# Causal zeroes written by GpSimd in place of mask products on TensorE, with a new order of a step

## The chip, the cores and the metric

The kernel runs on one core of a Trainium2 chip. A core has five engines with queues of their own: TensorE (PE in the profile, its weight loads as PEld), VectorE (DVE), ScalarE (ACT), GpSimd (POOL) and SyncE (SP, which here only starts DMAs). They wait for each other by semaphores. The metric is the device time of one execution in microseconds, lower is better. The time before is the median of three runs, 595.81 us (594.65 to 596.34).

## The reference

Eight sequences of 256 tokens with 128 channels go through a block of two attentions and a mixture of experts:

```python
x = _layernorm(x + _L0_attn_ref(x, Wq, bq, Wk, bk, Wv, bv, Wo, bo))     # attention A
x = _layernorm(x + _L0_ffn_ref(x, ...))                                 # attention B, then experts

# attention A: 16 query heads of 8 channels, one key head, one value head
att = jnp.einsum('bthd,bThd->bhtT', q, k) / math.sqrt(HD)
causal = jnp.triu(jnp.ones((Tx, Tx), bool), 1)
att = jnp.where(causal, -jnp.inf, att)
att = jax.nn.softmax(att, axis=-1)
out = jnp.einsum('bhtT,bThd->bthd', att, v).reshape(Bx, Tx, Cx)
return out @ Wo + bo
```

Attention B has 16 query heads of 64 channels and 4 key and value heads, also causal. The experts (8, the two best of each token routed, with a capacity) follow it. Only the causal mask of attention A is touched by the change: a key later than its query must get the probability 0.

## The kernel before

**Steps and stages.** The eight sequences go through a software pipeline of twelve steps, numbered -4 to 7. A step holds pieces of up to eight stages, each for another sequence: PA (projections and rotation of attention A), MA (row maxima of its scores), SA (its scores, exponentials and values), TA (its output, residual and norm), and PB, MB, SB and TB, which do the like for attention B. Steps 0 to 3 hold nearly all of them; PA ends with step 3, MA and SA with step 4, PB with step 5. The twelve steps end at about 500 us; a loop over 15 groups of expert tiles follows.

**Attention A of one sequence.** The score matrix of 256 x 256 per head is cut into three blocks, keys by queries: DIAG0 (the first 128 keys and queries), OFF (first keys, last queries), DIAG1 (last keys and queries). Later keys exist only in DIAG0 and DIAG1. `maxima_a` computes the masked scores with the queries on partitions, twelve tiles `am0` to `am11`, and VectorE reduces each to row maxima. `max_rows_a` transposes the maxima (`nm0`, `nm1`), ScalarE negates them, and a DMA writes them as an extra row of the query operand. `scores_a(s, c)` then computes block c transposed, keys on partitions, into all four banks of `ps_st`: four products of 25 rows (L700), one per group of four heads, that carry the negated maximum. For DIAG0 and DIAG1, four products of an identity with a key mask (L697) are accumulated ahead of them, which put -1e30 where the key is later. `exp_a` on ScalarE (L1691, two calls of 128 x 1024 per block, chunks 0 to 5) turns them into probabilities in `pt`; `values_a(s, 0)` (DIAG0) and `values_a(s, 1)` (OFF and DIAG1) multiply them with the values and a column of ones (L715).

**What sets the order.** Every engine's queue is written by hand in its function `step(s)`. TensorE's outputs other than scores go into a ring of four banks of `ps_r`, in the order of the table `ORDER`: each fill waits until the fill four places before it was read out by its reader, ScalarE or VectorE. So ORDER says both what TensorE does next and which reader it waits for. The names in it: `p00` to `p02` and `p10` to `p12` are the projections of attention B's queries and keys for the two halves of a sequence (L957), which VectorE's `rotate` reads; `r00` to `r12` their transposes (L966), which ScalarE's `high_parts` and then VectorE's `split` read; `bm0` to `bm11` the maxima tiles of attention B (L905, L909), `nmT` their transpose (L917); `bv0` to `bv3` its values (L930), `sm0`, `sm1` its weights (L946); `ax` and `qkv` the transposed input and projection of attention A (L670, L751); `av0`, `av1` the values of attention A (L715); `qT0`, `qT1`, `kT0`, `kT1` its transposed queries and keys (L765, L771); `xfT`, `lg` the router's (L813, L821).

**GpSimd.** Its queue per step: the product with the inverse sums (L592), `add_rotary` for both halves (L555, three additions each, one after each of `rotate`'s three parts), `spread_a` (L539 to L547, which `qT0` waits for) and copies.

Of the kernel before, what the change touches and what calls it, by code (L numbers as in the profile page):

```python
# [27 lines left out]
ALU = mybir.AluOpType  # L28
# [3 lines left out]
P = 128  # L32
# [156 lines left out]
def build(nc, x, Wq, bq, Wk, bk, Wv, bv, Wo, bo, g1, g2, wq, wk, wv, wo, router_w, router_b,  # L189
          w1, w2, w3, cf, cb, out):  # L190
    with ExitStack() as ctx:
# [192 lines left out]
        probs_a, probs_b = sem("probs_a"), sem("probs_b")  # L384
        xn_in = sem("xn_in")
# [134 lines left out]
        def _(pool):  # L520
# [35 lines left out]

            def scatter(i, lo, hi, src):
# [29 lines left out]
            for s in range(FIRST, NB):  # L587
# [7 lines left out]
                if "PB" in on:  # L595
                    add_rotary(s, 0)
                    add_rotary(s, 1)
                if "PA" in on:
                    spread_a(s + AHEAD["PA"])
                if s == FIRST:  # L600
# [45 lines left out]
        def _(pe):  # L646
# [38 lines left out]
            def scores_a(s, c):  # L685
# [10 lines left out]
                for a in range(4) if kind != OFF else ():  # L696
                    nc.tensor.matmul(o[a], ident_b, kmask.unsqueeze(1).broadcast_to([P, 4, P]), start=True, stop=False)  # L697
                for a in range(4):
                    rows = slice(RG * a, RG * a + NROW + 1)
                    mm = nc.tensor.matmul(o[a], kta[rows, a, P * kt:P * (kt + 1)], qta[rows, :, P * qt:P * (qt + 1)],  # L700
                                          start=kind == OFF, stop=True, tile_position=(RG * a, 0))
# [3 lines left out]
            def values_a(s, qt):  # L705
# [5 lines left out]
                pe.wait_ge(probs_a, E_A * n + (2 if qt == 0 else E_A))  # L711
                blocks = [(DIAG0, 0)] if qt == 0 else [(OFF, 0), (DIAG1, 1)]
# [257 lines left out]
            def step(s):  # L970
# [49 lines left out]
                if "PB" in on:  # L1020
                    project(s, 0)
                if s == NB - 1:
# [6 lines left out]
                else:  # L1029
                    values(s, 3)  # L1030
                    weights(s, 1)
                maxima_a(s, 10, 12)
                max_rows_a(s, 1)
                maxima(s, 8, 10)
                if "PB" in on:
                    project(s, 1)
                if "PA" in on:
                    n = s + AHEAD["PA"]
                    turn_x(s, "ax", x_all[:, NT * n:NT * (n + 1), :])
                if "SA" in on:  # L1040
                    scores_a(s, 0)
                maxima(s, 10, 12)
# [872 lines left out]
```

## Time and profile before

| what | value |
|---|---|
| median of three runs | 595.81 us (594.65 to 596.34) |
| the profiled execution, time / span | 594.53 us / 592.6 us |
| PE busy | 481.7 us (81%), 2788 instructions |
| DVE busy | 383.7 us (65%) |
| ACT busy | 229.4 us (39%) |
| POOL busy | 160.6 us (27%) |
| mean granted TensorE clock | 0.947 of full |
| chain that ended last | PE 56%, DVE 20%, ACT 12%, issue 4%, DMA 4%, POOL 3% |

The span runs from the first to the last instruction; 1.9 us of the time lie around it. A busy TensorE is not TensorE at its peak, since matmuls overlap. The granted clock has two levels, 1.2 and 2.4 GHz: 0.5 and 1.0 of full. The idle time of an engine that nobody waits for costs nothing, so what counts is who waited for whom, stretch by stretch.

### The profile page before, as it was taken

The numbers are of one execution on the slowest core, as the hardware profiler recorded it, in microseconds if no ns is written. First come the engines' busy times: TensorE is split into PE (matmuls) and PEld (weight loads), VectorE is DVE, ScalarE is ACT, GpSimd is POOL, SyncE is SP. The second block draws the span as 40 slices with busy tenths as digits, with TensorE's granted clock in tenths as the row PEclk, the third lists the DMA queues.
The fourth block names the chain that finished last, engine by engine and source line by source line (L and its number), as shares of the span: only waits on it lengthen the run. The fifth ranks groups of instructions, "written<-read, shape, count | busy, mean of one in ns | idle before, by whom it ended". The sixth has DMA issues, their size and how long they took to land.

```text
span 592.6 us, 8112 instructions
## 1 busy us (share of the span) xinstructions
PE 481.7 (81%) x2788; PEld 265.9 (45%) x2788; DVE 383.7 (65%) x1096; ACT 229.4 (39%) x420; POOL 160.6 (27%) x200
## 2 busy tenths in 40 slices
PE   3766686799979989997998799889967889898910
PEld 2423353355345535453653456344543535565610
DVE  3508678657857674857577666847678634675775
ACT  1251350374274238324641743264242232445400
POOL 4210601400323031324022420403223634033531
PEclk9977997899999999999999999989988989999965
DMA  7400000000002002100300030003043162013223
GB/s 212 148 1 1 1 1 2 2 1 1 3 3 71 2 3 52 23 2 2 73 2 2 2 73 2 2 3 71 2 144 72 47 147 72 2 59 98 70 50 85
DMA packets 19093, 23.82 MB, mean 40 GB/s; under 512 B 2630, under 2 KB 15374, under 8 KB 18158
## 3 DMA queue, kind: packets, MB, share of 16 engines
q1 hardware_dynamic: 15308, 18.19, 11.4%
q0 software_dynamic: 1648, 4.07, 2.7%
q10 hardware_dynamic: 2098, 1.05, 0.6%
q8 instruction: 23, 0.38, 0.3%
q14 instruction: 16, 0.13, 0.1%
HBM read 16.71 MB, written 6.28 MB: 39 GB/s over the span
## 4 chain that ended last, share of the span: by engine, by line
PE 56%; DVE 20%; ACT 12%; issue 4%; DMA 4%; POOL 3%; ACTq 1%; POOLq 0%; DVEq 0%; SPq 0%
PE ps_r L930 8%; PE ps_st L895 6%; ACT pt L1691 6%; PE ps_r L715 4%; PE ps_r L804 4%; PE ps_r L662 4%; PE ps_r L957 4%; PE ps_st L884 4%; DVE rmax L1194 4%; DVE rmax_a L1194 3%; PE ps_r L946 3%; DMA pt<-ys_dram,gidx 3%; PE ps_r L785 3%; POOL qkr L555 2%; PE ps_st L1096 2%
## 5 line engine op out<-in xcount | busy, mean ns | idle before, releaser
L555 POOL TENSOR_TENSOR qkr<-qkr,prod 128x512 f32<-128x512 f32 (+1 forms) x48 | 52.2, 1093 | 208.1 <-DVE prod L1310 207.0
L1194 DVE TENSOR_REDUCE rmax_a<-ps_r 128x2 f32<-128x512 f32 (+1 forms) x96 | 61.7, 686 | 26.1 <-PE ps_r L785 25.6
L662 PE MATMUL ps_r<-cbt 128*128 128x256 bf16 (+1 forms) x192 | 62.9, 327 | 4.9 <-DVE rmax_a L1194 2.4
L1194 DVE TENSOR_REDUCE rmax<-ps_r 128x2 f32<-128x512 f32 (+1 forms) x96 | 61.5, 684 | 4.9 <-PE ps_r L909 4.6
L592 POOL TENSOR_TENSOR oT<-pvb,oT 128x1024 f32<-128x1024 f32 x14 | 33.0, 2374 | 108.2 <-DMA oT<-inv_dram 108.2
L1700 ACT ACTIVATE pt<-ps_st 128x1024 f32<-128x1024 f32 x48 | 47.2, 1022 | 36.0 <-PE ps_st L895 36.0
L930 PE MATMUL ps_r<-pt,vb 128*64 128x512 f32 x192 | 48.9, 617 | 4.7 <-ACT pt L1700 3.0
L1691 ACT ACTIVATE pt<-ps_st 128x1024 f32<-128x1024 f32 x48 | 46.5, 1023 | 13.1 <-PE ps_st L700 12.8
L957 PE MATMUL ps_r<-wqkv,xT_b 128*128 128x512 f32 x96 | 47.6, 635 | 3.2 <-DVE rmax_a L1194 3.2
L785 PE MATMUL ps_r<-kq_a 128*128 128x512 f32 x96 | 46.7, 545 | 0.0
L1322 DVE TENSOR_TENSOR qbuf<-ps_r,qbuf 128x512 fp32r<-128x512 f32 x32 | 20.7, 687 | 34.1 <-ACT qbuf L1775 34.0
L1757 ACT ACTIVATE pvb<-ps_r 128x512 f32<-128x512 f32 x32 | 19.0, 595 | 59.3 <-PE ps_r L930 59.3
L662 PEld LDWEIGHTS ps_r<-cbt 128*128 128x128 bf16 x192 | 18.9, 98 | 48.6 <-issue 31.2
L895 PE MATMUL ps_st<-qbuf,kbuf 64*128 64x512 f32 x288 | 40.6, 415 | 0.0
L715 PE MATMUL ps_r<-pt,va 128*32 128x512 f32 x192 | 26.4, 655 | 9.3 <-ACT pt L1691 9.3
L895 PEld LDWEIGHTS ps_st<-qbuf,kbuf 64*128 64x128 f32 x288 | 25.9, 189 | 14.9 <-issue 10.6
L1307 DVE TENSOR_TENSOR qkr<-ps_r,cft 128x512 f32<-128x512 f32 (+1 forms) x48 | 28.5, 595 | 4.0 <-PE ps_r L957 4.0
L957 PEld LDWEIGHTS ps_r<-wqkv,xT_b 128*128 128x128 f32 x96 | 19.3, 206 | 22.3 <-issue 19.5
L909 PE MATMUL ps_r<-kbuf,qbuf 128*128 128x512 f32 x64 | 27.5, 488 | 0.0
L1248 DVE RECIPROCAL rda<-ps_r 128x16 f32<-128x16 f32 x16 | 4.0, 253 | 35.3 <-PE ps_r L728 35.3
L884 PE MATMUL ps_st<-nrow,cbt 128*128 128x512 bf16 x96 | 25.5, 389 | 1.3 <-DMA nrow<-negmax 1.3
L804 PE MATMUL ps_r<-wob,oT 128*128 128x128 f32 x224 | 26.4, 276 | 0.0
(237 smaller groups left out, 914.9 us busy)
## 6 DMA issues: line engine op xcount, KB each, us to landing
oT<-inv_dram SPq DMA_DIRECT2D x14, 512.0 KB, 6.3
xs_dram<-pvb SPq DMA_DIRECT2D x1, 2048.0 KB
pt<-in_L_ffn_w SPq DMA_DIRECT2D x2, 1024.0 KB, 7.2
ys_dram<-qkr SPq DMA_DIRECT2D x14, 128.0 KB
qkr<-xs_dram POOLq DMA_DIRECT2D x4, 256.0 KB, 5.8
x_all<-in_L_attn_x ACTq DMA_DIRECT2D x1, 896.0 KB, 6.3
pvb<-xs_dram POOLq DMA_DIRECT2D x3, 256.0 KB, 4.0
out<-x_all SPq DMA_DIRECT2D x1, 640.0 KB, 3.9
```

Of the source, the lines that this page charges most:

```text
L555: nc.gpsimd.tensor_tensor(part, part, prod[:, (3 * t + i) % 2, 0:w], ALU.add).then_inc(add_in, 1)
L662: nc.tensor.matmul(o[:, :, P * (i >= 4):], ident_b, qmask.unsqueeze(1).broadcast_to([P, heads, P]), start=True, stop=False, skip_group_che ...
L715: mm = nc.tensor.matmul(o[RG * a:RG * (a + 1), :], va[n % 2][:, kt, :], pt_a(kind)[:, 4 * a:4 * a + 4, :], start=i == 0, stop=i == len(blo ...
L785: nc.tensor.matmul(o, q, k, start=False, stop=True, skip_group_check=True).then_inc(full, 1)
L804: mm = nc.tensor.matmul(o[:, 0:C], of, wob[:, j, :], start=j == 0, stop=j == H // 2 - 1)
L884: nc.tensor.matmul(o[b], top_row if kind == OFF else add_row, nrow[:, G * hk:G * (hk + 1), P * qt:P * (qt + 1)], start=True, stop=False)
L895: mm = nc.tensor.matmul(o[b], k, q, start=False, stop=ql, tile_position=(DB * b, 0))
L930: mm = nc.tensor.matmul(o[DB * b:DB * (b + 1), :], vb[s % 2][:, kt, hk, :], pt_b(kind)[:, G * hk:G * (hk + 1), :], start=j == 0, stop=j == ...
L957: nc.tensor.matmul(o, xT_b[:, P * t:P * (t + 1)], wqkv[:, 512 * i:512 * (i + 1)], start=True, stop=True).then_inc(full, 1)
L1194: nc.vector.tensor_reduce(heads_of(i), ps_r[:, b, :].rearrange("p (h k) -> p h k", h=4 if i < 4 else 2), AX.X, ALU.max).then_inc(free[b], 1)
L1691: nc.scalar.activation(pt_a(kind)[:, 8 * half:8 * half + 8, :], ps_st[:, c % 2, :, :].rearrange("p b (h t) -> p (b h) t", h=4), ACT.Exp, s ...
L1700: nc.scalar.activation(pt_b(kind)[:, 8 * half:8 * half + 8, :], ps_st[:, c % 2, :, :].rearrange("p b (h t) -> p (b h) t", h=4), ACT.Exp, s ...
```

## The change

The eight mask products per sequence (L697, 64 in all) are left out; the first product of each bank now starts the accumulation. Two instructions of GpSimd per sequence, `affine_select` over 128 x 2048 elements in `pt`, keep a probability where the query index is at least the key index and write 0 elsewhere. They come after the exponentials of DIAG0 and of DIAG1 and before the values that read them, with a new semaphore `causal_in`. In GpSimd's queue the first stands between the two halves of `add_rotary`, the second behind `spread_a`.

The order of a step is changed with it: `scores_a(s, 0)` goes from behind `ax` to behind `p02`; `am10`, `am11` and `nm1` go ahead of `bv3` and `sm1`; `bm10`, `bm11` come together with `bm8`, `bm9` ahead of `p10`; `nmT` and `av0` stand ahead of `qkv`; and `av1` stands behind `kT1`, as the last of the step.

```diff
-         ("PB", "p00"), ("PB", "p01"), ("PB", "p02"), ("SB", "bv3"), ("SB", "sm1"),
...
+         ("PB", "p00"), ("PB", "p01"), ("PB", "p02"), ("MA", "am10"), ("MA", "am11"), ("SB", "bv3"), ("MA", "nm1"),
...
@@ gpsimd
+            def keep_causal(s, c):
+
+                pool.wait_ge(probs_a, E_A * (s + AHEAD["SA"]) + 2 * c + 2)
+                probs = pt_a(KINDS_A[c])
+                nc.gpsimd.affine_select(probs, probs, [[0, H], [1, P]], ALU.is_ge, 0.0, base=0, channel_multiplier=-1) \
+                    .then_inc(causal_in, 1)
+
...
                 if "PB" in on:
                     add_rotary(s, 0)
+                if "SA" in on:
+                    keep_causal(s, 0)
+                if "PB" in on:
                     add_rotary(s, 1)
                 if "PA" in on:
                     spread_a(s + AHEAD["PA"])
+                if "SA" in on:
+                    keep_causal(s, 2)
@@ tensor, scores_a
-                for a in range(4) if kind != OFF else ():
-                    nc.tensor.matmul(o[a], ident_b, kmask.unsqueeze(1).broadcast_to([P, 4, P]), start=True, stop=False)
...
-                                          start=kind == OFF, stop=True, tile_position=(RG * a, 0))
+                                          start=True, stop=True, tile_position=(RG * a, 0))
@@ tensor, values_a
                 pe.wait_ge(probs_a, E_A * n + (2 if qt == 0 else E_A))
+                pe.wait_ge(causal_in, 2 * n + 1 + qt)
@@ tensor, step
                     project(s, 0)
+                if "SA" in on:
+                    scores_a(s, 0)
+                maxima_a(s, 10, 12)
...
                     values(s, 3)
+                    max_rows_a(s, 1)
                     weights(s, 1)
-                maxima_a(s, 10, 12)
-                max_rows_a(s, 1)
-                maxima(s, 8, 10)
+                maxima(s, 8, 12)
...
                     turn_qk(s, 1)
+                if "PA" in on:
+                    turn_qk_a(s)
                 if "SA" in on:
                     values_a(s, 1)
-                if "PA" in on:
-                    turn_qk_a(s)
@@ vector, step
-                maxima(s, 8, 10)
+                maxima(s, 8, 12)
                 if "PB" in on:
                     rotate(s, 1)
-                maxima(s, 10, 12)
@@ scalar, step
+                if "SA" in on:
+                    exp_a(s, 0)
+                    exp_a(s, 1)
                 take_values(s, 3)
...
+                neg_max_a(s, 1)
                 take_weights(s, 1)
-                neg_max_a(s, 1)
+                if "MB" in on:
+                    neg_max(s)
```

The line numbers of the changed kernel are 11 or 12 higher from `scores_a` on: L710 is L700, L726 is L715, L968 is L957, L674 is L662, L1205 is L1194.

**The middle of a step.** TensorE's queue in step 1 before, from the last product of `bm9` over `p10` to `p12`, `ax`, the first scores of attention A, `bm10`, `bm11` and `nmT`:

```order
L909 MATMUL ps_r<-kbuf,qbuf 128x512
L957 MATMUL ps_r<-wqkv,xT_b 128x512 x3
L670 MATMUL ps_r<-cft,x_all 128x128 x2
L697 MATMUL ps_st<-cbt 128x512 x4
L700 MATMUL ps_st<-kq_a 128x512 x4
L662 MATMUL ps_r<-cbt 128x2x128
```

And in the changed kernel, in the same step, from `p00` to `p02` over the first scores, `am10`, `am11`, `bv3` and `nm1` to `sm1`:

```order
L968 MATMUL ps_r<-wqkv,xT_b 128x512 x3
L710 MATMUL ps_st<-kq_a 128x512 x4
L674 MATMUL ps_r<-cbt 128x2x128
L796 MATMUL ps_r<-kq_a 128x512
L674 MATMUL ps_r<-cbt 128x2x128
L796 MATMUL ps_r<-kq_a 128x512
L941 MATMUL ps_r<-pt,vb 64x512 x4
L803 MATMUL ps_r<-cft,rmax_a 16x128
L957 MATMUL ps_r<-pt,cft 32x512 x8
```

The scores now follow the first half's projections and have no mask products ahead of them.

VectorE's queue before, at the end of `rotate` for the second half:

```order
L1310 TENSOR_TENSOR prod<-ps_r,cft 128x8x32
L1306 COPY qkr<-ps_r 128x256
L1307 TENSOR_TENSOR qkr<-ps_r,cft 128x256
L1309 TENSOR_TENSOR prod<-ps_r,cft 128x4x32
L1310 TENSOR_TENSOR prod<-ps_r,cft 128x4x32
L1194 TENSOR_REDUCE rmax<-ps_r 128x2 x2
L1232 TENSOR_TENSOR flat<-ps_r,cft 128x272
```

In the changed kernel, at the start of the same `rotate`:

```order
L1404 SCALAR_TENSOR_TENSOR xf<-y,root_t_r,g2b 128x128 x2
L1205 TENSOR_REDUCE rmax<-ps_r 128x2 x4
L1318 TENSOR_TENSOR qkr<-ps_r,cft 128x512
L1320 TENSOR_TENSOR prod<-ps_r,cft 128x8x32
L1321 TENSOR_TENSOR prod<-ps_r,cft 128x8x32
```

All four reductions of `bm8` to `bm11` now stand ahead of `rotate`; before, two of them stood behind it.

**The end of a step.** TensorE's queue before, from the router's last product to the next step's first (L966 are `r10` to `r12`, L715 is `av1`, L765 and L771 are `qT0` to `kT1`, L884 opens the scores of attention B):

```order
L823 MATMUL ps_r<-bias,ones 128x8
L966 MATMUL ps_r<-cft,qkr 128x128 x10
L715 MATMUL ps_r<-pt,va 32x512 x8
L765 MATMUL ps_r<-cft,flat 128x128 x8
L771 MATMUL ps_r<-cft,kz 128x128 x8
L884 MATMUL ps_st<-nrow,cbt 128x512 x4
```

And in the changed kernel:

```order
L834 MATMUL ps_r<-bias,ones 128x8
L977 MATMUL ps_r<-cft,qkr 128x128 x10
L776 MATMUL ps_r<-cft,flat 128x128 x8
L782 MATMUL ps_r<-cft,kz 128x128 x8
L726 MATMUL ps_r<-pt,va 32x512 x8
L895 MATMUL ps_st<-nrow,cbt 128x512 x4
```

`av1` has moved behind the four transposes, so the next step's first scores stand right behind it.

**GpSimd.** Its queue in step 1 before:

```order
L592 TENSOR_TENSOR oT<-pvb,oT 128x1024 x2
L555 TENSOR_TENSOR qkr<-qkr,prod 128x512 x2
L555 TENSOR_TENSOR qkr<-qkr,prod 128x256
L555 TENSOR_TENSOR qkr<-qkr,prod 128x512 x2
L555 TENSOR_TENSOR qkr<-qkr,prod 128x256
L539 TENSOR_TENSOR flat<-qkr_a,hr 128x32x8
L542 COPY flat<-hr 128x32x8 x2
L546 COPY kz<-hr 128x8x8 x2
L547 TENSOR_TENSOR kz<-qkr_a,hr 128x8x8
L611 COPY vb<-qkr 128x512
```

And in the changed kernel:

```order
L555 TENSOR_TENSOR qkr<-qkr,prod 128x256
L561 AFFINE_SELECT pt<-pt 128x2048
L555 TENSOR_TENSOR qkr<-qkr,prod 128x512 x2
L555 TENSOR_TENSOR qkr<-qkr,prod 128x256
L539 TENSOR_TENSOR flat<-qkr_a,hr 128x32x8
L542 COPY flat<-hr 128x32x8 x2
L546 COPY kz<-hr 128x8x8 x2
L547 TENSOR_TENSOR kz<-qkr_a,hr 128x8x8
L561 AFFINE_SELECT pt<-pt 128x2048
L623 COPY vb<-qkr 128x512
```

The two selects are new; nothing else of GpSimd's moved against each other.

## Rows read from the trace of the kernel before

**Rows 1.** The page: busy time and share of each engine; granted clock in 40 slices.
```profile
PE 481.7 (81%) x2788; PEld 265.9 (45%) x2788; DVE 383.7 (65%) x1096; ACT 229.4 (39%) x420; POOL 160.6 (27%) x200
...

```

**Rows 2.** Windows, step 1: length, busy of PE, PEld, DVE, ACT, POOL, clock, DMA.
```profile
176.30:231.80 55.50, 50.24 (x311) 27.40 (x310) 37.91 (x103) 25.10 (x48) 14.16 (x16) 1.00 0.09 21
```

**Rows 3.** Groups by form, the mask products: busy us, mean ns, idle before.
```profile
L697 PE MATMUL ps_st<-cbt 128*128 128x512 bf16 x64 | 16.7, 384 | 7.8 <-ACT pt L1691 7.8
```

**Rows 4.** TensorE's timeline in step 1: start us, us, instructions [idle before <-releaser].
```profile
203.68 2.81 PE L957 MATMUL ps_r<-wqkv,xT_b 128*128 128x512 f32 x6 [0.80 <-DVE rmax_a L1194]
206.42 1.94 PE L930 MATMUL ps_r<-pt,vb 128*64 128x512 f32 x8
...
212.14 0.27 PE L792 MATMUL ps_r<-cft,rmax_a 128*16 128x128 f32 x1 [1.12 <-DVE rmax_a L1194]
...
215.74 1.03 PE L697 MATMUL ps_st<-cbt 128*128 128x512 bf16 x4
216.70 0.51 PE L700 MATMUL ps_st<-kq_a 25*128 25x512 f32 x4
...
219.72 0.27 PE L917 MATMUL ps_r<-cft,rmax 128*32 128x128 f32 x1 [1.70 <-DVE rmax L1194]
219.84 0.48 PE L751 MATMUL ps_r<-wa,xT_a 128*128 128x144 f32 x2
...
224.51 1.04 PE L697 MATMUL ps_st<-cbt 128*128 128x512 bf16 x4 [0.87 <-ACT pt L1691]
...
228.17 1.92 PE L715 MATMUL ps_r<-pt,va 128*32 128x512 f32 x16 [0.45 <-ACT pt L1691]
230.03 1.09 PE L765 MATMUL ps_r<-cft,flat 128*128 128x128 f32 x8
...
231.83 1.03 PE L884 MATMUL ps_st<-nrow,cbt 128*128 128x512 bf16 x4
```

**Rows 5.** VectorE's timeline in step 1.
```profile
208.91 0.28 DVE L1310 TENSOR_TENSOR prod<-ps_r,cft 128x128 f32<-128x128 f32 x1
...
213.22 1.28 DVE L1194 TENSOR_REDUCE rmax<-ps_r 128x2 f32<-128x512 f32 x2
...
218.09 0.28 DVE L1310 TENSOR_TENSOR prod<-ps_r,cft 128x128 f32<-128x128 f32 x1
```

**Rows 6.** ScalarE's timeline in step 1.
```profile
222.52 1.94 ACT L1691 ACTIVATE pt<-ps_st 128x1024 f32<-128x1024 f32 x2
...
227.91 1.10 ACT L1775 ACTIVATE qbuf<-ps_r 128x512 fp32r<-128x512 f32 x2
228.86 0.78 ACT L1779 ACTIVATE kbuf<-ps_r 64x256 fp32r<-64x256 f32 x2
```

**Rows 7.** GpSimd's groups by form.
```profile
L555 POOL TENSOR_TENSOR qkr<-qkr,prod 128x512 f32<-128x512 f32 x32 | 40.6, 1276 | 207.0 <-DVE prod L1310 207.0
L592 POOL TENSOR_TENSOR oT<-pvb,oT 128x1024 f32<-128x1024 f32 x14 | 33.0, 2374 | 108.2 <-DMA oT<-inv_dram 108.2
...
L542 POOL COPY flat<-hr 128x256 f32<-128x256 f32 x16 | 5.9, 398 | 0.0
...
L611 POOL COPY vb<-qkr 128x512 f32<-128x512 f32 x8 | 4.9, 610 | 0.1
```

**Rows 8.** TensorE's timeline in steps -3, -2, 4 and 5.
```profile
34.22 1.26 PE L697 MATMUL ps_st<-cbt 128*128 128x512 bf16 x4 [2.10 <-ACT pt L1691]
...
38.33 3.58 PE L715 MATMUL ps_r<-pt,va 128*32 128x512 f32 x16 [2.12 <-ACT pt L1691]
...
70.32 1.06 PE L715 MATMUL ps_r<-pt,va 128*32 128x512 f32 x8 [1.26 <-ACT pt L1691]
...
386.17 0.27 PE L917 MATMUL ps_r<-cft,rmax 128*32 128x128 f32 x1 [1.92 <-DVE rmax L1194]
...
434.02 0.27 PE L917 MATMUL ps_r<-cft,rmax 128*32 128x128 f32 x1 [3.37 <-DVE rmax L1194]
```

More of the change, by code:

```diff
@@ L384, in build @@
         probs_a, probs_b = sem("probs_a"), sem("probs_b")
+        causal_in = sem("causal_in")
         xn_in = sem("xn_in")
@@ L1030, in step @@
                     values(s, 3)
+                    max_rows_a(s, 1)
                     weights(s, 1)
-                maxima_a(s, 10, 12)
-                max_rows_a(s, 1)
-                maxima(s, 8, 10)
+                maxima(s, 8, 12)
                 if "PB" in on:
                     project(s, 1)
+                if "MB" in on:
+                    max_rows(s)
                 if "PA" in on:
@@ L1040, in step @@
                 if "SA" in on:
-                    scores_a(s, 0)
-                maxima(s, 10, 12)
-                if "MB" in on:
-                    max_rows(s)
+                    values_a(s, 0)
                 if "PA" in on:
@@ L1049, in step @@
                 if "SA" in on:
-                    values_a(s, 0)
                     scores_a(s, 1)
@@ L1395, in step @@
                     ins.then_inc(xf_in, 1)
-                maxima(s, 8, 10)
+                maxima(s, 8, 12)
                 if "PB" in on:
                     rotate(s, 1)
-                maxima(s, 10, 12)
                 if "PA" in on:
@@ L1822, in step @@
                     inverse_root(root_t, var_t, ln_t, r0_t, NB)
+                neg_max_a(s, 1)
                 take_weights(s, 1)
-                neg_max_a(s, 1)
+                if "MB" in on:
+                    neg_max(s)
                 if "PA" in on:
@@ L1827, in step @@
                 if "SA" in on:
-                    exp_a(s, 0)
-                    exp_a(s, 1)
-                if "MB" in on:
-                    neg_max(s)
+                    take_values_a(s, 0)
                 if "TB" in on and s < NB - 1:
@@ L1834, in step @@
                 if "SA" in on:
-                    take_values_a(s, 0)
                     exp_a(s, 2)
@@ L1844, in step @@
                     high_parts(s, 1)
-                if "SA" in on:
-                    take_values_a(s, 1)
                 if "PA" in on:
@@ L1849, in step @@
                     turned_a(s, "kT", kta)
+                if "SA" in on:
+                    take_values_a(s, 1)
             def weigh(lo, hi, count):
```

9 rows, old and new, of the table ORDER are left out of this document.

## The prediction

> **What bounds the kernel now.** Read three views, from wide to narrow. The page first: TensorE is busy for 81% of the span, and its clock is at full in the slices of the middle steps and below it in some of the early ones and of the tail [rows 1]. The windows next: in step 1, TensorE is busy for 50.2 of 55.5 us at a clock of 1.00, VectorE for 37.9, GpSimd for 14.2 [rows 2]. So steps 0 to 3 look bound by TensorE, and whatever leaves its queue should come off the time. The timeline shows what the shares hide: the last third of a step is a braid. TensorE waits there for VectorE before `nm1` (1.12 us) and before `nmT` (1.70), and for ScalarE before the third scores (0.87) and `av1` (0.45) [rows 4]. These are the places that the change touches, so it is these waits that say how much of a removed product is a gain.
>
> **The mask products.** There are 64, in 16 groups of four. A group starts 0.96 us before the scores that follow it (215.74 to 216.70, [rows 4]), so 16 x 0.96 = 15.4 us leave TensorE's queue; the group's line has 16.7 us of busy time, since matmuls overlap [rows 3]. That is the upper end of the gain, if no other engine is next.
>
> **The selects.** What adds 16 instructions to GpSimd is cheap for the engine, 27% busy [rows 1], but no row shows `affine_select`. Bounds for 128 x 2048: the copies take 398 ns for 256 elements and 610 for 512, so 0.83 ns per element and 0.61 + 1536 x 0.00083 = 1.9 us; the two-input products take 1276 ns for 512 and 2374 for 1024, so 2.14 ns per element and 2.37 + 1024 x 0.00214 = 4.6 us [rows 7]. A select reads one tensor as a copy does, so I take 2.0 us, call it X, and keep 1.9 to 4.6. The first select of a step stands behind `add_rotary` of the first half, and has until `av0`, some 8 us; it is hidden for any X. The second select is not: it can start only after the last exponential of DIAG1, and `av1` needs it.
>
> The Trainium skill, page "GPSIMD Engine Reference", section "Performance pitfalls for Q7 kernels", speaks against my X: a compare-and-select loop that isn't unrolled costs 2.03 cycles per element, unrolled 1.03. An estimate by that page with its 1.2 GHz is 3.5 us or 1.8 us; the sum below would then be near -1 us or -9 us. No row here shows which.
>
> **The middle of a step (step 1).** I replay the queues with the durations of the rows. `p02` ends and `bv3` starts at 206.4 [rows 4]. The new queue: first scores until 206.8 (0.43), `am10` and `am11` until 207.7, a short wait for `p01`'s bank, `bv3` until 209.8. `nm1` needs the maxima of `am10`, `am11`, which VectorE starts when `rotate` of the first half ends at 209.2 [rows 5] and ends 1.2 later: 210.5. `sm1` (1.85) until 212.5, `bm8` to `bm11` (0.36 each) until 214.0, the second half's projections (2.7, as the first half's from 203.68 [rows 4]) until 216.7. VectorE waits for `bm8` until 213.0, does the four reductions (0.60 each) until 215.4 and `rotate` (it started 1.20 after 213.22 and ended at 218.37, so 3.95 [rows 5]) until 219.4. `qkv` takes the bank of `p12`, so it starts at 219.5; before it did so at 219.84 [rows 4]. So the first mask group, the shorter wait at `nm1` and the vanished wait at `nmT` bring 0.3 us together, not 1 to 3: VectorE's `rotate` is next, and it now has two more reductions ahead of it. In step 0, which lacks the router's work, the same working gives 0.1 us later than before.
>
> **The end of a step.** Counted from the start Q of `qkv`. ScalarE is the bound: its exponentials of OFF started at Q + 2.7 and the six read-outs of the second half's transposes at 5.4 us behind them [rows 6]. Now `av0` is no longer between, and the exponentials start at Q + 1.6; the chain of exponentials (1.8), read-outs (1.8), exponentials (1.8) brings the last exponential's end to Q + 7.1, the read-outs to Q + 7.0 to 8.7 and VectorE's last split 1 us later, Q + 9.7. `qT1`, `kT0` and `kT1` take the banks of `r10` to `r12`, so `kT1` ends at Q + 10.2 in place of the earlier end of `av1`; `av1` (1.86) comes last. It starts at Q + 10.2 or Q + 7.2 + X, whichever is later, and ends at Q + 12.1 for X up to 3.0. Before, the step ended at 231.83, Q + 12.0 [rows 4]. So the second mask group gains nothing in steps 1 to 3 either: what TensorE saves, it waits for banks. Sum for steps 0 to 3: +0.1 - 3 x 0.25 = -0.7 us. Beyond X = 3.0 each of these steps loses X - 3.0, since the select delays `av1`, and behind it the next step's scores.
>
> **The other steps.** Here the order pays. Step -2: the exponentials of DIAG0 were waited for (1.26 us at 70.32 [rows 8]); with the scores ahead of the second half's projections that is hidden, and by the same replay the step ends 1.7 us earlier. Step -1: `qkv` is freed of the wait for VectorE and comes 1.7 us earlier, and so does the end. Step 4 has no `qkv`: the scores of OFF can follow `av0` at once, 3.7 us earlier; the last part is then bound by ScalarE and the select, and ends at 393.0 + X against 396.94 before: -2.1 at X = 1.9, and TensorE no longer waits 1.92 us for VectorE at `nmT` [rows 8]. Step 5 has no attention A scores, but the wait of 3.37 us at `nmT` [rows 8] goes, since the four reductions are ahead of `rotate`; `rotate` is late instead and holds `r01`: -1.8. Step -3 has nothing to hide the selects behind, and its waits for exponentials are 2.10 and 2.12 us [rows 8]; both X lie on the path: with 5 us less of waits and masks than before and 2 X more, -1.4 at X = 1.9. From step 5 on nothing else changes and the shift is carried to the end.
>
> **The sum** at X = 1.9: -1.4 - 1.7 - 1.7 - 0.7 - 2.1 - 1.8 = -9.4; at X = 2.0 it is -9.1. The slope is 3 us per us of X up to 3.0 (step -3 twice, step 4), then 9 (steps -2 to 3 as well): -6.1 at 3.0, 0 near 3.7, +8 at 4.6. The sum goes against the profiled execution's 594.53 us (span 592.6 and 1.9 around it): 585.4. That execution is 1.3 us below the median of 595.81, so for a median I say 587.0.
>
> **Rivals.**
> *TensorE is the bound after all.* If my hand replay puts too much behind VectorE and ScalarE, the 15.4 us come off whole, and step 5's 1.8: 578.6. For it: 50.2 of 55.5 us busy [rows 2]. Against it: the waits in exactly these stretches [rows 4].
> *The select is slow.* X at 4.6, the two-input row: `av1` waits 1.6 us in each of steps -2 to 3, more in -3: 595.8 + 8 = 604, slower than before; it decides from X = 3.7 on. For it: the select also makes an index and compares. Against it: one input.
> *The gains cancel.* X of 3.3 to 3.9, or the clock. TensorE's clock fell to its lower level, 1.2 GHz, after waits: `av1` of step -3 took 3.58 us in place of 1.92 after two waits of 2.1 us [rows 8]. At the end of a step TensorE now has some 1.9 us of waits before `qT1` to `kT1`, so the clock could fall there, and the four score products and `av1` behind would take some 2 us more; in four steps that is 8 us and leaves 594 to 597. Against it: single waits of 1.70 us left the clock at 1.00 [rows 2, 4]. The Trainium skill, page "TensorE: Matmul & The Clock Gate", section "HAM oscillation — how this bites in real kernels", says that recurring waits bring the clock down in every round; by it the time would be in this case, and the row at 38.33 agrees.
> *The change does nothing to the path*: the early steps gain, but the tail, bound by routing, waits for other things; then some 594. Nothing in the rows speaks for it.
>
> **Chances.** Forecast (select near a copy, 583 to 591): 0.50. TensorE is the bound (577 to 583): 0.12. Cancelled (591 to 598): 0.23. Slow select (598 to 606): 0.15. A run can tell about 0.3%, 1.8 us, from no change. Faster: 0.50 + 0.12 + 0.06 of the cancelled = 0.68; same 0.12; slower 0.05 + 0.15 = 0.20. The range from 580 to 600 leaves out some 0.17 of the ends.
>
> **What would show it.** The select's duration, 1.9 to 3.0 us. Step 1's `qkv` some 13.1 us behind the end of `p02`, with VectorE's `rotate` as the releaser; waits of TensorE before `qT1` and `kT1` for VectorE; `av1` waiting for GpSimd not at all in steps 0 to 3, by about 1 to 3 us in step 4; no wait at `nmT` anywhere; steps 1 to 3 still near 55.3 us; clock 1.00 there. I am wrong if steps 1 to 3 take below 54.5 (TensorE was the bound) or above 56 (select or clock).

## The result, and the profile after

The changed kernel takes 604.58 us (median of four runs, 602.17 to 607.69) against 596.08 us for the kernel before: 1.0149 of its time, 95% interval 1.0098 to 1.0200. It is slower by some 1.5%, where the forecast was 587.0 us and the range ended at 600. Its profiled execution took 602.17 us, with a span of 600.3 us against 592.6 us. The ratios here and below leave out the slow runs, those over 1.5% above the fastest of their kernel, and are not the quotients of the medians beside them, from which they differ by up to 0.7%.

The page of the changed kernel, beside [rows 1]: the 64 products are gone (2788 to 2724), yet TensorE is busy for longer. The second line is the granted clock in 40 slices, the third the same of the kernel before.

```profile
PE 486.5 (81%) x2724; PEld 264.8 (44%) x2724; DVE 387.3 (65%) x1096; ACT 231.5 (39%) x420; POOL 193.4 (32%) x216
...
PEclk9957987889989999999799999979988989999965
...
PEclk9977997899999999999999999989988989999965
```

The line of the selects among GpSimd's groups, beside [rows 7]:

```profile
L561 POOL TENSOR_SCALAR_AFFINE_SELECT pt<-pt 128x2048 f32<-128x2048 f32 x16 | 32.1, 2004 | 29.2 <-ACT pt L1701 29.2
```

X, the price of one select, is 2.0 us, the value taken. So the forecast did not fall with its most doubtful number. Where the span grew shows in the starts of the steps, each taken from TensorE's timeline at the first product of attention B's scores:

| start of step | 0 | 1 | 2 | 3 | 4 | 5 | 6 | 7 | end |
|---|---|---|---|---|---|---|---|---|---|
| before, us | 126.1 | 176.3 | 231.8 | 287.3 | 342.8 | 396.9 | 438.9 | 475.0 | 592.6 |
| after, us | 127.7 | 179.6 | 235.1 | 292.2 | 347.6 | 401.7 | 443.5 | 481.8 | 600.3 |
| later by | 1.6 | 3.3 | 3.2 | 4.8 | 4.8 | 4.8 | 4.5 | 6.8 | 7.7 |

The windows of the changed kernel, steps 0 to 4 (columns as in [rows 2], the clock ahead of the last two):

```profile
127.70:179.60 51.90, 46.72 (x265) 22.86 (x261) 33.94 (x88) 24.71 (x43) 13.06 (x15) 0.97 0.02 3
179.60:235.10 55.50, 49.92 (x306) 26.51 (x303) 38.66 (x103) 25.30 (x46) 18.10 (x18) 1.00 0.09 20
235.10:292.20 57.10, 52.25 (x306) 28.33 (x303) 39.53 (x103) 25.40 (x46) 18.10 (x18) 0.94 0.10 22
292.20:347.60 55.40, 49.82 (x305) 26.44 (x301) 38.23 (x103) 25.39 (x46) 18.11 (x18) 1.00 0.08 19
347.60:401.70 54.10, 48.16 (x281) 24.19 (x277) 37.70 (x97) 22.62 (x41) 16.08 (x12) 0.96 0.09 21
```

Steps 1 and 3 take 55.4 us at a clock of 1.00, as long as before [rows 2]: 8 products fewer, and nothing off the time. Steps 0 and 2 hold the same work as before and as their neighbour, but at 0.97 and 0.94, and each is some 1.7 us longer than the kernel before needed (50.3 and 55.5 us). TensorE's timeline at the end of step 1 and of step 2 shows one and the same row of instructions at the two levels of the clock, beside [rows 4]:

```profile
229.33 0.63 PE L776 MATMUL ps_r<-cft,flat 128*128 128x128 f32 x4
231.25 0.66 PE L776 MATMUL ps_r<-cft,flat 128*128 128x128 f32 x4 [1.30 <-DVE qbuf L1333]
231.85 1.42 PE L782 MATMUL ps_r<-cft,kz 128*128 128x128 f32 x8
233.20 1.92 PE L726 MATMUL ps_r<-pt,va 128*32 128x512 f32 x16
235.06 0.82 PE L895 MATMUL ps_st<-nrow,cbt 128*128 128x512 bf16 x3
...
284.95 1.06 PE L776 MATMUL ps_r<-cft,flat 128*128 128x128 f32 x4
286.69 1.11 PE L776 MATMUL ps_r<-cft,flat 128*128 128x128 f32 x4 [0.67 <-DVE qbuf L1333]
287.60 1.91 PE L782 MATMUL ps_r<-cft,kz 128*128 128x128 f32 x8
289.44 2.79 PE L726 MATMUL ps_r<-pt,va 128*32 128x512 f32 x16
```

`av1` (L726) needs 1.92 us in step 1 and 2.79 in step 2, part of it at 1.2 GHz. In step -3, where little else runs beside the selects, and in step 4, the selects stand on the path as well; the middle line is the wait of the products that read `av1`'s result, at the start of step -2:

```profile
29.81 1.94 PE L726 MATMUL ps_r<-pt,va 128*32 128x512 f32 x8 [1.79 <-POOL pt L561]
...
44.27 1.06 PE L739 MATMUL ps_r<-cft,pvs 128*128 128x128 f32 x8 [0.80 <-ACT pvs L1753]
...
398.15 3.64 PE L726 MATMUL ps_r<-pt,va 128*32 128x512 f32 x16 [2.73 <-POOL pt L561]
```

In step 4 the wait for the select is 2.73 us, within the 1 to 3 us foreseen, and the `av1` behind it takes 3.64 us in place of 1.92: the wait is paid twice.

### The profile page after: what moved, and what is told of

It reads as the page before. It is cut to its first block, busy times and chain, and to the rows that moved or that the text cites. A ratio compares the mean times of both kernels' runs of the same rounds, so it can differ in the third digit from the quotient of the medians.

```text
span 600.3 us, 8009 instructions
## 1 busy us (share of the span) xinstructions
PE 486.5 (81%) x2724; PEld 264.8 (44%) x2724; DVE 387.3 (65%) x1096; ACT 231.5 (39%) x420; POOL 193.4 (32%) x216
## 4 chain that ended last, share of the span: by engine, by line
PE 49%; DVE 24%; ACT 10%; issue 6%; POOL 5%; DMA 5%; ACTq 1%; POOLq 0%; DVEq 0%; SPq 0%
PE ps_st L906 6%; PE ps_r L941 6%; ACT pt L1701 5%; PE ps_r L815 4%; PE ps_st L895 4%; PE ps_r L674 4%; PE ps_r L726 4%; DVE rmax L1205 4%; POOL qkr L555 3%; DMA pt<-ys_dram,gidx 3%; DVE rmax_a L1205 3%; PE ps_r L796 2%; DVE qkr L1318 2%; PE ps_r L957 2%; PE ps_st L1107 2%
## 5 line engine op out<-in xcount | busy, mean ns | idle before, releaser
L1205 DVE TENSOR_REDUCE rmax_a<-ps_r 128x2 f32<-128x512 f32 (+1 forms) x96 | 61.8, 686 | 21.1 <-PE ps_r L796 20.7
L674 PE MATMUL ps_r<-cbt 128*128 128x256 bf16 (+1 forms) x192 | 63.7, 332 | 4.2 <-DVE rmax_a L1205 2.3
L1205 DVE TENSOR_REDUCE rmax<-ps_r 128x2 f32<-128x512 f32 (+1 forms) x96 | 60.9, 684 | 5.2 <-PE ps_r L920 4.3
L968 PE MATMUL ps_r<-wqkv,xT_b 128*128 128x512 f32 x96 | 46.8, 626 | 3.8 <-DVE rmax_a L1205 3.2
L561 POOL TENSOR_SCALAR_AFFINE_SELECT pt<-pt 128x2048 f32<-128x2048 f32 x16 | 32.1, 2004 | 29.2 <-ACT pt L1701 29.2
L674 PEld LDWEIGHTS ps_r<-cbt 128*128 128x128 bf16 x192 | 19.0, 99 | 48.3 <-issue 32.0
L726 PE MATMUL ps_r<-pt,va 128*32 128x512 f32 x192 | 30.2, 742 | 8.5 <-POOL pt L561 4.7
L1333 DVE TENSOR_TENSOR qbuf<-ps_r,qbuf 128x512 fp32r<-128x512 f32 x32 | 20.8, 687 | 20.8 <-ACT qbuf L1785 20.7
L906 PEld LDWEIGHTS ps_st<-qbuf,kbuf 64*128 64x128 f32 x288 | 26.1, 191 | 15.6 <-issue 11.2
L895 PE MATMUL ps_st<-nrow,cbt 128*128 128x512 bf16 x96 | 27.2, 410 | 3.1 <-DMA nrow<-negmax 3.1
L968 PEld LDWEIGHTS ps_r<-wqkv,xT_b 128*128 128x128 f32 x96 | 18.8, 205 | 22.6 <-issue 16.4
L977 PE MATMUL ps_r<-cft,qkr 128*128 128x128 f32 x160 | 25.2, 293 | 3.7 <-DVE prod L1321 2.3
```

The lines of the kernel that those rows point to most:

```text
L674: nc.tensor.matmul(o[:, :, P * (i >= 4):], ident_b, qmask.unsqueeze(1).broadcast_to([P, heads, P]), start=True, stop=False, skip_group_che ...
L726: mm = nc.tensor.matmul(o[RG * a:RG * (a + 1), :], va[n % 2][:, kt, :], pt_a(kind)[:, 4 * a:4 * a + 4, :], start=i == 0, stop=i == len(blo ...
L895: nc.tensor.matmul(o[b], top_row if kind == OFF else add_row, nrow[:, G * hk:G * (hk + 1), P * qt:P * (qt + 1)], start=True, stop=False)
L906: mm = nc.tensor.matmul(o[b], k, q, start=False, stop=ql, tile_position=(DB * b, 0))
L968: nc.tensor.matmul(o, xT_b[:, P * t:P * (t + 1)], wqkv[:, 512 * i:512 * (i + 1)], start=True, stop=True).then_inc(full, 1)
L1205: nc.vector.tensor_reduce(heads_of(i), ps_r[:, b, :].rearrange("p (h k) -> p h k", h=4 if i < 4 else 2), AX.X, ALU.max).then_inc(free[b], 1)
```

## The experiments

Two theories went in. **Waits**: each of the three parts (order, masks, selects) moves waits, and those add up. **Clock**: the mask products, useless as work, kept TensorE's clock at its upper level through the waits around them; without them it falls. The kernels were run in four batches (x, y, z, w; y and w on one chip, x and z on two others), each batch with the kernel before, and the ratios are to that. x1, x3, z3 and z4 leave out the causal mask of attention A, so their results are not the reference's. In batches y and w the kernel before itself had medians of 599.5 and 600.3 us, so times of different batches are not compared.

**The parts one by one.** x1 takes the masks out of the kernel before; x2 has the new order, masks, no selects; x3 has the new order and neither; x4 is the changed kernel with more work for TensorE ahead of `qT1`'s wait. y1 is the changed kernel with the mask products put back as well.

```diff
# x1: before, without
-                for a in range(4) if kind != OFF else ():
-                    nc.tensor.matmul(o[a], ident_b, kmask..., start=True, stop=False)
# x2, x3: after, without
-                    keep_causal(s, 0)
-                    keep_causal(s, 2)
-                pe.wait_ge(causal_in, 2 * n + 1 + qt)
# x4: after, qT0's four transposes issued four times
+                    for b in 4 * list(range(4)) if t == 0 else range(4):
```

> The kernel before, in its old order, without the 64 mask products and without selects (later keys keep their probabilities, so the causal mask of attention A is left out). Theory A (the end of a step is bound by ScalarE's exponentials and the banks, the middle by VectorE, so TensorE's saving turns into waits): steps 0 to 3 keep their 50.3 and 55.5 us, only steps -3 to -1 and 4 gain some 1 us each; 591 to 594 us. Rival B (TensorE is the bound, and it is the new order that lost the gain): 15 us off, 580 to 583 us.

> The new order with the 64 mask products kept and no selects: the reordering alone. If the order and the clock behind it are the loss (theory A: TensorE waits at the end of a step, its clock falls to the lower level, av1 behind it takes 2.7 to 3.6 us in place of 1.9), this stays slower than before, 599 to 605 us. If the selects are the loss (rival C), it is at or below before, 590 to 596 us.

> The changed kernel without its 16 selects (the causal mask is left out). The difference from the changed kernel's 604.6 us is the whole price of the selects. Theory A: they are on the path only in steps -3 and 4 (and by 2.7 us there): 598 to 601 us. Rival C (each second select delays av1): below 594 us.

> The changed kernel with the four transposes of qT0 done four times over (12 more transposes of 128 x 128 per sequence, some 1.3 us of TensorE each step, 96 in all), in front of the wait of 1.5 us before qT1. Theory A (the waits at the end of a step let the clock fall): the clock stays at 1.00 in steps -1 to 3, av1 goes back to 1.9 us, and the time falls in spite of more work, to 599 to 602 us. Rival (the clock has nothing to do with these waits): the same 604.6 us, or up to 10 us more.

| kernel | median, us | ratio to before (95%) |
|---|---|---|
| x1, old order, no masks, no selects | 601.35 | 1.0114 (1.0071 to 1.0157) |
| x2, new order, masks, no selects | 582.73 | 0.9811 (0.9788 to 0.9833) |
| x3, new order, no masks, no selects | 596.28 | 1.0035 (1.0004 to 1.0067) |
| x4, after, `qT0` repeated | 599.13 | 1.0118 (1.0092 to 1.0144) |

The first three went against what I expected of them, and together they turn the case over. The order alone is worth 1.9%, and taking the products out costs time in either order: 1.1% in the old one, some 2.3% in the new one. x1's trace shows how. Its step 3, in TensorE's timeline:

```profile
331.31 0.37 PE L915 MATMUL ps_r<-cft,rmax 128*32 128x128 f32 x1 [2.13 <-DVE rmax L1192]
331.47 0.78 PE L749 MATMUL ps_r<-wa,xT_a 128*128 128x144 f32 x2
...
333.42 1.94 PE L713 MATMUL ps_r<-pt,va 128*32 128x512 f32 x8
335.29 0.80 PE L698 MATMUL ps_st<-kq_a 25*128 25x512 f32 x4
```

The product that is gone has become a longer wait for VectorE at `nmT`, 2.13 us where [rows 4] has 1.70, and behind it everything runs at half speed: `av0` (L713) takes 1.94 us for eight products that took 1.07 before, the four score products 0.80 in place of 0.51. Nearly the same wait, 2.12 us, in its step 1 left the clock up, and that step took 55.5 us; steps 2 and 3 took 56.5 and 57.5. So the fall is not certain at any one wait; it becomes likelier.

In x4 the repeated transposes cover the wait at `qT1`, and in its profile (span 593.5 us) the clock is at 1.00 in steps 0, 2 and 3; but that execution was among the shortest of six (594.3 to 601.7 us), and the ratio of all six, 1.0118, is hardly below what the changed kernel itself has (1.0124 and 1.0149). By its time x4 settles nothing; its trace has what I expected of `av1`, 1.92 to 1.93 us in all steps from -3 to 3.

**Old order with selects.** y2 keeps the old order, in which `av1` is followed by `qT0` to `kT1`, and gives it the selects, without the mask products; the first select stands there behind `add_rotary` of both halves.

> The changed kernel, selects and order as they are, with the 64 mask products back (they are superfluous: both mask the same keys, and the result is the reference's). Theory A (without the products TensorE waits more, its clock falls to 1.2 GHz at the ends of the steps and half-speed products cost more than the removed ones): adding 16 us of products takes time off, 604.6 us on the chip of the first comparison becomes 586 to 592 us. Rival (what the changed kernel loses is the selects' waits, and the products only cost): 604 us or more.

> The masking alone in the old order: no mask products, 16 selects, the first behind add_rotary of the second half, the second behind spread_a. Correct result, so no other tokens go to the experts than before. The run without products and selects in this order took 601.4 us. Theory A: the same loss to the clock, and av1 in its old place waits some 2 us for each second select: 606 to 616 us. Rival (the 601.4 us came from the unmasked data, not from the clock): 593 to 603 us.

y2 takes 647.84 us, 1.0820 (1.0701 to 1.0939), far beyond what I had reckoned. TensorE's timeline at the end of its step 1:

```profile
251.37 3.64 PE L726 MATMUL ps_r<-pt,va 128*32 128x512 f32 x16 [2.73 <-POOL pt L562]
254.95 1.87 PE L776 MATMUL ps_r<-cft,flat 128*128 128x128 f32 x8
```

Steps 1 to 3 end as step 4 of the changed kernel does, with a wait of 2.73 us and an `av1` at half speed, and `qT0` and `qT1` behind it take 1.87 us in place of 1.09 [rows 4]: a step takes some 61.6 us at a clock of 0.91 to 0.92. `av0` waits for no select in step 1. In the changed kernel `av1`, as the last of the step, waits for none in these steps, as the forecast had it. That its place is what makes the selects bearable fits these rows, but no run moves `av1` alone with the selects in.

y1 (600.42 us, 1.0086, 1.0036 to 1.0137) stayed above my range, by the ratio as well. The masks back in, its steps 0 to 3 run at 1.00, 1 to 3 in 55.4 us each, but step 4 is hardly helped (53.6 against 54.1 us). The medians of all runs of this batch (599.48 for the kernel before) give 1.0016, and so does the repeat in batch z.

**The clock, with the data held fixed.** z4 is the sharpest test: x3 with the mask products issued, each of them closed and then overwritten by the scores, so that it computes what x3 computes and differs in TensorE's load alone.

```diff
# z4: x3, and ahead of the scores of DIAG0 and DIAG1
+                    nc.tensor.matmul(o[a], ident_b, kmask..., start=True, stop=True)
```

> The changed kernel once more, beside the three below, since chips and runs differ by some us: ratio to before 1.010 to 1.020 as in the first comparison.

> The changed kernel with the mask products kept beside the selects, once more. Theory A (the products keep the clock up at the ends of the steps): below the run without them by 4 to 8 us, ratio 1.000 to 1.009. Rival (the earlier difference was between chips): the same ratio as the run without them.

> New order, no mask products, no selects (the causal mask of attention A is left out), once more: ratio 1.000 to 1.007, with runs apart by up to 8 us according to the step in which the clock falls.

> As the run before and with the same data, but the 64 mask products are issued and then overwritten by the score products (start=True on both), so the causal mask of attention A is left out here too, and only TensorE's work differs. With the products as real masks this order gave 0.981. Theory A (their work keeps the clock): 0.978 to 0.985. Rival (the unmasked data sends other tokens to the experts and costs the time): as the run before, 1.000 to 1.007.

All four in one batch (before: 594.74 us):

| | mask products gone | mask products issued |
|---|---|---|
| **no selects** | z3: 596.25, 1.0021 (0.9987 to 1.0055) | z4: 584.68, 0.9826 (0.9769 to 0.9883) |
| **selects** | z1: 603.88, 1.0124 (1.0074 to 1.0175) | z2: 596.49, 1.0016 (0.9985 to 1.0048) |

16.5 us of dead work on TensorE take 11.6 us off the time. `av1`, always the same 16 products, shows step by step where the clock was down (us, from the timelines; 1.92 is full speed):

| step | -3 | -2 | -1 | 0 | 1 | 2 | 3 | 4 | step 0 starts at |
|---|---|---|---|---|---|---|---|---|---|
| before | 3.58 | 1.92 | 1.92 | 1.92 | 1.92 | 1.92 | 1.92 | 1.92 | 126.1 |
| changed kernel | 2.37 | 2.06 | 3.42 | 2.69 | 1.92 | 2.79 | 1.92 | 3.64 | 127.7 |
| the same again (z1) | 2.12 | 2.81 | 1.92 | 2.02 | 2.86 | 1.92 | 2.88 | 3.51 | 126.7 |
| z3 | 2.64 | 2.18 | 3.56 | 2.79 | 1.92 | 2.84 | 1.92 | 2.42 | 124.5 |
| z4 | 1.92 | 1.93 | 1.92 | 1.92 | 1.92 | 1.92 | 1.92 | 1.92 | 119.0 |

One window over steps 0 to 4, z3's first, then z4's:

```profile
124.50:395.30 270.80, 246.38 (x1445) 128.98 (x1441) 181.49 (x493) 123.49 (x222) 63.73 (x71) 0.97 0.08 17
```
```profile
118.90:386.10 267.20, 247.45 (x1485) 128.99 (x1481) 182.81 (x492) 122.36 (x222) 63.78 (x71) 1.00 0.08 18
```

z4 does 40 products more in 3.6 us less, at 1.00 against 0.97. The spans of the two executions differ by 11.2 us, 594.0 against 582.8. Half of it, 5.5 us, lies ahead of step 0, where the mean granted clock is 0.88 and 0.94; 2.9 lie in step 6. The groups by form show the same instructions at two prices, z3's values of attention A and then z4's, with the added products:

```profile
L721 PE MATMUL ps_r<-pt,va 128*32 128x512 f32 x192 | 28.8, 711 | 3.8 <-DVE prod L1316 3.6
```
```profile
L705 PE MATMUL ps_st<-cbt 128*128 128x512 bf16 x64 | 16.5, 380 | 7.8 <-ACT pt L1698 7.0 <-DMA kq_a<-nega 0.8
...
L723 PE MATMUL ps_r<-pt,va 128*32 128x512 f32 x192 | 23.9, 600 | 4.6 <-DVE prod L1318 4.1 <-ACT pt L1698 0.5
```

711 ns against 600 ns for one product, 192 times: 21 us of product time, of which the overlap of products leaves 4.9 us of busy time in this line alone. The clock theory is shown: with the data and the order held fixed, the added products bring the clock up and the time down, and steps at 1.00 take 55.4 us with them and without. The first table also gives the selects' price, 1.0 to 1.9% (z3 and z4 compute on unmasked data, but x2, with real masks, had 0.9811 beside z4's 0.9826), and that the two harms overlap: either alone brings the time from 0.983 to 1.002, both together only to 1.012.

**Which select, and what kind of filler.** w1 and w2 keep one select each, with the masks; w3 is the changed kernel with each score product of a diagonal block issued three times (25 rows, not 128).

```diff
# w1: after with masks, without
-                    keep_causal(s, 2)
# w2: after with masks, without
-                    keep_causal(s, 0)
# w3: after
+                for i, a in enumerate(list(range(4)) if kind == OFF else 3 * list(range(4))):
...
```

> New order with the mask products and only the first select of each sequence (DIAG0, ahead of av0). No select gave a ratio of 0.982, both gave 1.002. The first is on TensorE's path in step -3 alone, where it has no rotary additions and projections beside it: 2 to 4 us, 0.985 to 0.989. Rival (it also delays GpSimd's additions for the second half in every step): 0.993 or more.

> New order with the mask products and only the second select (DIAG1, ahead of av1). It is on the path in step -3 and in step 4, where TensorE waited 2.7 us for it and its clock fell behind the wait: 6 to 9 us, 0.992 to 0.998. Rival (hidden like the first): 0.983 to 0.987.

> The changed kernel, correct, with the four score products of DIAG0 and DIAG1 issued three times over (each overwrites the one before), 128 more products of 25 rows, some 0.9 us per block as the mask products took. If any work of TensorE in that place keeps the clock, the ratio is that of the kernel with both masks, 1.000 to 1.006. If it takes products over all 128 rows, it stays at the changed kernel's 1.012 to 1.015.

w1: 0.9844 (0.9766 to 0.9923). w2: 0.9943 (0.9896 to 0.9990). Against x2's 0.9811, another batch's, the first select costs some 0.3% and the second some 1.3%; the first figure is not clear of the intervals, while the second select's being the dearer holds within the batch. In w1's trace the first select costs nothing in steps 1 to 4, but step 0 starts 3.9 us later than in x2's. w2's trace has the second one in steps -3 and 4, where x2's `av1` takes 1.92 us without a wait, or behind one of 0.45 us:

```profile
39.41 3.44 PE L727 MATMUL ps_r<-pt,va 128*32 128x512 f32 x16 [2.31 <-POOL pt L561]
...
391.93 3.64 PE L727 MATMUL ps_r<-pt,va 128*32 128x512 f32 x16 [2.53 <-POOL pt L561]
```

Step 4 takes 54.1 us in place of x2's 50.3, about half of the 3.8 us being the wait and half the clock; in step -3 it is 2.3 us. w3 gives 1.0057 (1.0027 to 1.0087) where the changed kernel has 1.012 to 1.015, and its steps 1 to 3 take 55.4 to 55.6 us at 1.00. In its step 0 the clock fell all the same (0.97, `av1` 3.39 us), as it did in z2 with the real masks (0.97, 3.19 us). So products with 25 rows do for the clock what the masks did beside the selects, as far as one execution of each shows, and it is TensorE's being fed that counts, not the mask.

**Better than both.** Since the order was the gain, y3 takes x2 and puts `av1` back ahead of `qT0` (without a select it need not be last), and y4 also moves the second half's projections ahead of `sm1` and `bm8` to `bm11`, and `nmT` behind `qkv`, so that VectorE's `rotate` starts earlier. w4 is y4 again, in another batch.

```diff
# y3, ORDER (and the queues alike)
-         ("PA", "qT0"), ("PA", "qT1"), ("PA", "kT0"), ("PA", "kT1"), ("SA", "av1")]
+         ("SA", "av1"), ("PA", "qT0"), ("PA", "qT1"), ("PA", "kT0"), ("PA", "kT1")]
# y4, besides
+         ("PB", "p10"), ("PB", "p11"), ("PB", "p12"), ("SB", "sm1"), ("MB", "bm8"), ..., ("MB", "bm11"),
+         ("PA", "ax"), ("SA", "av0"), ("PA", "qkv"), ("MB", "nmT"), ...
```

> The new order with mask products and no selects, with av1 back in its old place ahead of qT0. TensorE has work there in place of the wait for r10's bank. Theory A: each step from -2 to 3 ends some 0.8 us sooner and the turned values no longer wait 0.8 us: 577 to 581 us. Rival (the end is bound by ScalarE alone): 582 to 584 us.

> As the run before, and the second half's projections p10 to p12 ahead of sm1 and bm8 to bm11, so that VectorE's rotate of the second half no longer stands behind four reductions; nmT behind qkv. Theory A (VectorE's idle 1.3 us before bm8 is on the path to qkv): qkv comes 1.2 to 1.4 us sooner in steps 0 to 3: 572 to 577 us. Rival (the four reductions only move the wait to qkv): as the run before, within 2 us.

> The fastest version so far once more, since the kernel before spread over 11 us on the chip of its first comparison (mask products, no selects, first scores early, av1 ahead of qT0, second half's projections ahead of sm1): ratio to before 0.966 to 0.980.

y3: 583.57 us, 0.9755 (0.9638 to 0.9872). The time is above the one expected, but so was the kernel before in this batch; of the 593.35 us of batch x the ratio makes 578.8, and in its trace steps 1 to 3 take 54.1 us where x2's step 3 takes 55.4. y4: 580.07 us, 0.9707 (0.9575 to 0.9839), above the 572 to 577 us expected, though its step 2 takes 52.9. w4: 582.39 us, 0.9680 (0.9592 to 0.9768). The window of step 2 in w4, a full step in 52.8 us with all its products at 1.00:

```profile
221.00:273.80 52.80, 50.27 (x312) 27.39 (x310) 38.03 (x103) 25.03 (x47) 14.18 (x16) 1.00 0.09 22
```

50.27 us busy, as before [rows 2]; 2.7 us of waits have gone. This is the best version found, 3% below the kernel before, and it keeps the mask products.

## Why the prediction was wrong

The span was to be 9.1 us shorter and is 7.7 us longer. (The forecast's own numbers make 586.7 for a median; 587.0 is rounded up.) By its own steps, in us of span (X = 2.0):

| part | predicted | measured |
|---|---|---|
| steps -3 to -1 | -4.6 | +1.6 |
| steps 0 to 3 | -0.7 | +3.2 |
| step 4 | -2.0 | 0.0 |
| step 5 | -1.8 | -0.3 |
| steps 6, 7 and the groups behind | 0 | +3.2 |

**Right.** X, 2.0 us. The replay of the middle of a step: `qkv` starts 13.1 us behind the end of `p02` (222.84 against 209.71), with VectorE's last product of `rotate` as releaser. The end: 12.2 us behind the start of `qkv` (235.06), 12.1 foreseen; TensorE waits at `qT1` for VectorE's split. So in steps 1 and 3 the two mask groups bring nothing, as the sum says. Neither "TensorE is the bound" nor "the select is slow" came true.

**Wrong: the clock, put among "the gains cancel" and left out of the sum.** The mechanism was named at one right place, the end of a step, with 2 us for each of four steps, more than was lost there; it was given part of a chance of 0.23 and set aside since "single waits of 1.70 us left the clock at 1.00". That inference failed. In the trace of the kernel before itself, a single wait of 1.92 us at `nmT` in step 4 [rows 8] has an `av0` at half speed close behind it, 1.94 us for the eight products that take 1.07 in step 1 [rows 4]:

```profile
386.73 1.94 PE L715 MATMUL ps_r<-pt,va 128*32 128x512 f32 x8
```

In x1 single waits of 2.1 us did the same in three steps of four. And several short waits, with less work between them, brought the clock down in some steps and not in others. In step 0 of the changed kernel TensorE waits 0.78, 0.41 and 1.50 us within 6 us, and `av1` then takes 2.69 us. Steps 0 and 2 lose 1.7 us each in this way, which is the +3.2. The Trainium skill, page "TensorE: Matmul & The Clock Gate", section "A second HAM failure mode: psum-queue depth-cycling", tells of a kernel whose TensorE idles briefly but often between groups and so swings between the levels; these rows agree, and I had weighed only the long waits of the section ahead of it.

**Wrong: a removed product was costed at nothing at worst.** The forecast asked what 15.4 us less work could gain and found little; it never asked what the products did in their place. z4 against z3 has the answer: putting them back is worth 11.6 us. The lower end of that term should have been below zero, and the row at 38.33 [rows 8], an `av1` at half speed behind two waits, was the hint.

**Wrong: the early steps, the largest part, and step 4.** Of the 16.8 us between the forecast and the measured span, 6.2 lie in steps -3 to -1, 3.9 in steps 0 to 3 and 2.0 in step 4. In steps -3 to -1 `av1` takes 2.37, 2.06 and 3.42 us, where z4 has 1.92 and the kernel before 3.58, 1.92 and 1.92: the clock is down at the end of each of them, and the forecast had put a price on that in four steps only, and outside the sum. Without the selects, issuing the products brings the start of step 0 from 124.5 to 119.0 us (z3, z4); with them, from 126.7 to 124.6 (z1, z2). The wait for the select in step 4 was foreseen (2.73 us), the `av1` of 3.64 us behind it was not: +1.7 of the 2.0. Its start was right: 50.5 us into the step, where the forecast's end less the 1.86 us of `av1` gives 50.3. `av1` is now TensorE's last fill, and in steps -2 and -1 the products that turn its result (L739) stand right behind it, so they wait 0.8 us for ScalarE's copy in each of the two; before, `qT0` to `kT1` covered it. I had replayed the step up to `av1`, not what is queued behind it. x2 waits there as well, so this belongs to the new order. The first select stands on the path in step -3 (1.79 us), as foreseen. Without selects and with masks (x2) step 0 starts 5.4 us earlier than before, more than the 4.6 us of the forecast.

**Mis-sized: step 5.** The wait of 3.37 us at `nmT` has gone, but the step is only 0.3 us shorter (1.2 in x2): smaller waits for VectorE came in its place, and the clock is 0.95 against 0.96.

**The tail.** Step 7 starts behind a wait of 3.07 us for the DMA of attention B's negated maxima, where the kernel before waited 1.28, and the groups behind it run at 0.87 against 0.88. This isn't the change's doing alone: x3 and its repeat z3, one and the same kernel, wait 1.30 and 3.39 us there, and their step 6 takes 35.0 and 40.4 us. What sets it is open, and with it the 3.2 us of this part. It is part of why single executions of one kernel spread by 1 to 2% here.

**Both harms at once.** x2 has a span of 584.0 us, 8.6 less than before, close to the 9.1 that I had forecast for the whole. That closeness is partly chance: the 9.1 count 4 us of selects in step -3 and the 15.4 us of products gone, and by parts x2 has -5.4, +0.7, -3.9, -1.2 and +1.1 where the forecast has -4.6, -0.7, -2.0, -1.8 and 0. The order is the gain; the selects (some 1 to 2%) and the missing products (1 to 2%) took it back and more.

## What to carry to other kernels

A product that an engine does in the shadow of others' waits is free, and may be what holds TensorE's clock up: before work is taken off TensorE, ask whether the place is bound by it, and put a loss, not only zero, at the end of the range. A change that mixes a new order, new work on another engine and removed work should be run in its parts, since here the best part (0.981) was hidden by the two others. A wait just ahead of a long group of products costs twice where the clock falls: 2.7 us of waiting brought 1.7 us of slower products.

## What the chip showed that I had not expected

**Dead work that pays.** 64 products of 0.38 us, overwritten at once, take 11.6 us off (z4 against z3, 0.9826 against 1.0021), and repeated products of 25 rows seem to do so in part (w3, 1.0057, against 1.012 to 1.015 in other batches).

**The same row of work at either level.** Steps 1 and 2 of the changed kernel have the same 306 products and nearly the same waits, and take 55.4 and 57.1 us. In another execution of the same kernel (z1) it is the other way round: steps 1 and 3 take 57.2 us and step 2 takes 55.4. What tips the one and not the other is not settled by these runs.

**VectorE held by a select.** VectorE's first product of the Newton step of TB's norm, 128 x 2 with both inputs in SBUF, among its groups, first in x2 and then in the changed kernel; the third and fourth lines are one of them in VectorE's timeline of the changed kernel, and the select in GpSimd's:

```profile
L1164 DVE TENSOR_TENSOR root_t_a<-root_t_r 128x2 f32<-128x2 f32 x8 | 1.2, 152 | 1.0 <-ACT root_t_r L1729 1.0
```
```profile
L1167 DVE TENSOR_TENSOR root_t_a<-root_t_r 128x2 f32<-128x2 f32 x8 | 7.3, 907 | 1.0 <-ACT root_t_r L1732 1.0
...
213.60 1.66 DVE L1167 TENSOR_TENSOR root_t_a<-root_t_r 128x2 f32<-128x2 f32 x1
...
213.24 2.00 POOL L561 TENSOR_SCALAR_AFFINE_SELECT pt<-pt 128x2048 f32<-128x2048 f32 x1
```

An instruction of 0.15 us takes 1.66 and ends with the select, at 215.3: it is held until the select is through. The instructions of VectorE that read PSUM beside the second select (L1333, 1.29 us for two, with and without selects) are not held. The Trainium skill, page "SBUF — State Buffer", section "SBUF: two separate sides", says that an instruction of VectorE with two inputs in SBUF and one of GpSimd that reads SBUF lock a shared pair of ports against each other for the whole instruction; the trace agrees. Here it cost 6.1 us of VectorE's time and next to nothing on the path in step 1, since VectorE was through with the rest at 216.4, as `bm8` came; what it costs ahead of a reduction that is waited for, no run shows.
